# Attention's rows of maxima loaded by ACT itself, with one load moved ahead in the QKV queue and the routing's picks taken in two parts

## The chip, the cores and the metric

One core of one Trainium2 chip runs the whole program. The metric is the device time of one execution in microseconds (us). A measurement of this kernel can tell a difference of about 1% from no change.

## The reference

All arithmetic is float32. Input x is (4, 512, 512): 2,048 tokens of 512 features.

```python
x = x + 0.5 * ffn(layernorm(x))      # 8 experts, the best 2 by gate logits, relu(x W_e + b_e), mean of the two
x = x + attention(layernorm(x))      # 32 heads of 16, ALiBi bias, causal softmax, then Wout
x = x + 0.5 * ffn(layernorm(x))      # the same experts again

# attention: qkv = clip(x Wqkv^T, -8, 8); q, k = layer_norm(q), layer_norm(k)
# scores = q k^T / 4 + slope * (k_pos - q_pos), masked above the diagonal; softmax; times v; times Wout^T
# ffn: logits = x W_gate + b_gate; top 2 experts of 8; mean of relu(x W_e + b_e) over the two
```

## The kernel before, in words

The order of work on every engine is written out by hand; each engine has one queue of instructions, and semaphores order them across engines. SP issues the plain transfers, POOL the indirect ones (gather of token rows, scatter-add of results). Stages in order of time: routing 1 with the weights' split into high and low parts (about 0 to 88 us), experts 1 (to 235), QKV projection (to 430), attention (to 720), routing 2 with the output projection (to 836), experts 2.

**QKV** goes over 16 tiles of 128 tokens. In tile t DVE (`unit`, L478) first takes the statistics of x of tile t+2 (L485), so it waits for that tile's load. SP's `step` (L310) for tile t does three things in order: `store_qk(t-2)` (L301, four stores of 256 KB), `load_x(t+3)` (L293, 256 KB), `store_v(t)` (L297, 512 KB). From tile 8 to 11 each step is followed by `load_fixed` and `load` (L207, L218), which bring the q and k stacks of one of attention's first four groups (14 transfers).

**Attention** goes over 32 groups n of 4 heads, and in each over five units u. PE computes scores twice: query-major two groups ahead (`scores`, L715), of which DVE takes row maxima (`reduce`, `combine`); and key-major (`scores_by_key`, L746), of which ACT takes exponentials (`exps`, L851). The maxima enter the key-major product as extra rows of the q stack: POOL splits them into high and low parts (`split_max`, L666), PE turns them (`turn_max`, L737), ACT copies them to SBUF (`copy_max`, L845, behind the second unit's exponentials), and SP moves them by four transfers of 4 KB into two rows in each half of the stack (`max_rows`, L631). `scores_by_key(n+1, 0)` waits for these transfers (L749). In SP's loop over n (L648) stand, in order: the stack's load for group n+4, the values' load for n+2, `max_rows(n+1)`, every second time the store of results, and in groups 16 to 24 an early transfer for routing 2 (`route.sync_early`, L660, mostly 512 KB of expert weights).

**Routing** normalises eight pairs of tiles (DVE), transposes them (PE, L1295; ACT copies, L1390), multiplies by the gate (PE `gate`, L1302), adds the bias (ACT `logits_out`, L1395) and turns the logits to one PSUM bank (PE `turn_logits`, L1311). When all 16 tiles are there, DVE picks the two experts by a chain of 16 dependent instructions over 128 columns (L1492 to L1507); PE then ranks the tokens (L1362), DVE computes the slots, and the experts' gathers start.

Of the kernel before, what the change touches and what calls it, by code (L numbers as in the profile page):

```python
# [12 lines left out]
F32 = mybir.dt.float32  # L13
# [217 lines left out]
def qkv_block(nc, block, st, x1, w_turned, w_out, wo_stage, ln_params, q_dram, k_dram, v_dram):  # L231
# [4 lines left out]
    with ExitStack() as ctx:  # L236
# [334 lines left out]
def attention_block(nc, block, st, last_turns, freed, route, oT, wo_stage, v_dram, o_dram, wo_turned):  # L571
# [4 lines left out]
    with ExitStack() as ctx:  # L576
# [4 lines left out]
        part = [m.sb(f"part{i}", [P, 2, 2, SEGS]) for i in range(2)]  # L581
        m_parts = [m.sb(f"m_parts{i}", [P, 2, 4, SEGS], F32R) for i in range(2)]
        m_rows = [m.sb(f"m_rows{i}", [2 * HG, SEQ], F32R) for i in range(2)]
# [22 lines left out]
        wo_tr, wo_out = m.sem("wo_tr"), m.sem("wo_out")  # L606
        STACK_LOADS, FIXED_LOADS = 8, 6

        def ring_unit(k):

            return s_ps[k % 2]
# [4 lines left out]
        @block.sync  # L616
        def _(sp):
            def load(n):
                at_least(sp, st_done, T_UNITS * (n - SLOTS + 1))
                if n == AHEAD:  # L620
                    for par in range(2):
                        sp.wait_ge(st.v_stored[par], 16 * (TILES // 2))
                        sp.wait_ge(st.qk_stored[par], STORES * (TILES // 2))
                st.load(sp, n)

            def load_v(n):
                at_least(sp, pv_done, n - RING + 1)
# [19 lines left out]
            max_rows(0)  # L647
            for n in range(NG):  # L648
                if n + AHEAD < SLOTS:
                    st.load_fixed(sp, n + AHEAD)  # L650
                if n + AHEAD < NG:
                    load(n + AHEAD)
                if n + 2 < NG:
                    load_v(n + 2)
                if n + 1 < NG:
                    max_rows(n + 1)
                if n >= 3 and n % 2 == 1:
                    store(n - 2)
                if NG // 2 <= n < NG // 2 + EARLY_LOADS:
                    route.sync_early(sp, n - NG // 2)  # L660
            route.sync_next(sp)
            store(NG - 1)

        @block.gpsimd
        def _(pool):
            def split_max(n):  # L666
                pool.wait_ge(comb_done, n + 1)
                at_least(pool, mT_done, n - 1)
                flat = part[n % 2][:, :, :, :].rearrange("p a b s -> p (a b) s")
                nc.gpsimd.tensor_copy(m_parts[n % 2][:, 0, :, :], flat).then_inc(m_hi_done, 1)  # L670
                pool.wait_ge(m_hi_done, n + 1)
                nc.gpsimd.tensor_tensor(m_parts[n % 2][:, 1, :, :], flat, m_parts[n % 2][:, 0, :, :].bitcast(F32),
                                        ALU.subtract).then_inc(m_lo_done, 1)
# [30 lines left out]
        def _(pe):  # L704
# [32 lines left out]
            def turn_max(n):  # L737
                pe.wait_ge(m_lo_done, n + 1)
                bank = ring_unit(6 * (n + 1) + 1)
                at_least(pe, red_done, S_UNITS * (n + 1))  # L740
                for i, seg in enumerate((0, 4, 6, 5)):
                    last = nc.tensor.matmul(bank[0:2 * HG, i * P:(i + 1) * P], m_parts[n % 2][:, :, :, seg], ident_r[:, :],
                                            start=True, stop=True)
                last.then_inc(mT_done, 1)

            def scores_by_key(n, u):  # L746
                slot = n % SLOTS
                if u == 0:
                    pe.wait_ge(m_loaded[n % 2], 64 * (n // 2 + 1))  # L749
                e = 2 * (T_UNITS * n + u)  # L750
# [94 lines left out]
        def _(act):  # L845
            def copy_max(n):
                act.wait_ge(mT_done, n + 1)
                at_least(act, m_loaded[n % 2], 64 * (n // 2))
# [15 lines left out]

            copy_max(0)
            for r in range(C):
                act.wait_ge(wo_tr, r + 1)
# [5 lines left out]
            for n in range(NG):  # L873
# [133 lines left out]
def route_block(nc, m, tables, ex, x_in, xn_dram, acc, w_gate, b_gate, w_e, b_e, freed=None, o_dram=None, wo_turned=None, o_rows=None,  # L1007
# [58 lines left out]
    lg_ps = t_ps[0] if proj else wq_ps[3]  # L1066
    lgT = work[0:E, 0:2 * P]
    root = route_ps[:, 0:4]
# [19 lines left out]
    slot_lo = tables.sb("slot_lo", [P, 2 * TILES])  # L1088
    at_col = tables.sb("at_col", [P, COL_RING, P], BF16)
    at_tile = tables.sb("at_tile", [P, 2 * TILES, 3, TAB], BF16)  # L1090
# [19 lines left out]
    ln_chain, chain_sem = m.sem("ln_chain"), m.sem("chain")  # L1110
    picked_done, rank_done, onehot_done, ids_done = (m.sem(n) for n in ("picked_done", "rank_done", "onehot_done", "ids_done"))
    token_done = m.sem("token_done")
    wo_hi_done, wo_lo_done = m.sem("wo_hi_done"), m.sem("wo_lo_done")
# [134 lines left out]
    def gpsimd(pool):  # L1248
# [9 lines left out]
        for n in range(TILES):  # L1258
            pool.wait_ge(w_hi_done, n + 1)
            if n == TILES - 1:  # L1260

                pool.wait_ge(picked_done, 1)
            nc.gpsimd.tensor_tensor(ex.w_lo[:, 2 * n:2 * n + 2, :], ex.w_lo[:, 2 * n:2 * n + 2, :].bitcast(F32),  # L1263
# [66 lines left out]
    def tensor(pe):  # L1330
        pe.wait_ge(ident_done, 1)
        pe.wait_ge(g_loaded, 16)
        for u in range(PAIRS + 2):
# [25 lines left out]
        pe.wait_ge(const_done, 12)  # L1359
        pe.wait_ge(picked_done, 1)  # L1360
        both = pair[:, :, :, :].rearrange("p t k e -> p (t k e)")
# [91 lines left out]
    def vector(dve):  # L1453
# [35 lines left out]
        dve.wait_ge(const_done, 12)  # L1489
        dve.wait_ge(gate_done, PAIRS)  # L1490
        three = [P, TILES, E]
        for k, source in enumerate((logits, rest)):  # L1492
            chain(nc.vector.tensor_reduce(best[:, :, 0], source[:, :, :], X_AXIS, ALU.max))
            chain(nc.vector.tensor_tensor(eq[:, :, :], source[:, :, :], best[:, :, :].to_broadcast(three), ALU.is_equal))
            chain(nc.vector.scalar_tensor_tensor(val[:, :, :], eq[:, :, :], -100.0, n_expert[:, :, :], ALU.mult, ALU.add))
            chain(nc.vector.tensor_reduce(low[:, :, 0], val[:, :, :], X_AXIS, ALU.min))
            chain(nc.vector.tensor_tensor(pick[k][:, :, :], val[:, :, :], low[:, :, :].to_broadcast(three), ALU.is_equal))
            if k == 0:

                chain(nc.vector.scalar_tensor_tensor(rest[:, :, :], pick[0][:, :, :], NEG, logits[:, :, :], ALU.mult, ALU.add))  # L1500


        chain(nc.vector.tensor_tensor(picked[:, :, :], pick[0][:, :, :], pick[1][:, :, :], ALU.add))
        chain(nc.vector.scalar_tensor_tensor(val[:, :, :], picked[:, :, :], -100.0, n_expert[:, :, :], ALU.mult, ALU.add))
        chain(nc.vector.tensor_reduce(low[:, :, 0], val[:, :, :], X_AXIS, ALU.min))
        chain(nc.vector.tensor_tensor(pair[:, :, 0, :], val[:, :, :], low[:, :, :].to_broadcast(three), ALU.is_equal))
        nc.vector.tensor_tensor(pair[:, :, 1, :], picked[:, :, :], pair[:, :, 0, :], ALU.subtract).then_inc(picked_done, 1)  # L1507

# [292 lines left out]
```

## Time and profile before

| what | value |
|---|---|
| median of 3 runs | 975.37 us (970.96 to 982.41) |
| the profiled execution: its time, its span | 983.81 us, 982.0 us |
| PE busy, DVE, ACT, POOL | 841.5 us (86%), 632.4 (64%), 449.1 (46%), 446.1 (45%) |
| SP's hardware queue | 95,328 packets, 126.40 MB, 46.6% of 16 DMA engines |
| mean granted TensorE clock | 0.923 |

The span runs from the first to the last instruction. PE's busy time is modelled from pipelined matmuls, so a share of 86% does not say that PE never waits. ACT issues no transfer in this kernel: the profile has SP's queue and POOL's. SP's transfer instructions are listed with engine SPq, and their duration is that of issuing, not of moving the data.

### The profile page before, as it was taken

The numbers are of one execution on the slowest core, as the hardware profiler recorded it, in microseconds if no ns is written. First come the engines' busy times: TensorE is split into PE (matmuls) and PEld (weight loads), VectorE is DVE, ScalarE is ACT, GpSimd is POOL, SyncE is SP. The second block draws the span as 40 slices with busy tenths as digits, with TensorE's granted clock in tenths as the row PEclk, the third lists the DMA queues.
The fourth block names the chain that finished last, engine by engine and source line by source line (L and its number), as shares of the span: only waits on it lengthen the run. The fifth ranks groups of instructions, "written<-read, shape, count | busy, mean of one in ns | idle before, by whom it ended". The sixth has DMA issues, their size and how long they took to land. (4 is left out here: it accounts for less than half of the span.)

```text
span 982.0 us, 18936 instructions
## 1 busy us (share of the span) xinstructions
PE 841.5 (86%) x5922; PEld 592.5 (60%) x5923; DVE 632.4 (64%) x1289; ACT 449.1 (46%) x834; POOL 446.1 (45%) x565
## 2 busy tenths in 40 slices
PE   3666999993989998878899999889989983899995
PEld 1344888872677777655455555445557752788874
DVE  7966344333978877776688887678728768344432
ACT  3541333332244443347577777577754430233331
POOL 7732677764022222224243344235446431577764
PEclk9785999996899999978899999899999995899998
DMA  9985677863264689665667679898239940578874
GB/s 341 387 300 175 124 148 145 149 118 53 54 197 150 196 199 230 195 196 127 146 139 154 143 154 189 165 192 178 54 107 321 323 161 32 123 144 152 149 133 62
DMA packets 113255, 164.54 MB, mean 168 GB/s; under 512 B 16929, under 2 KB 74401, under 8 KB 112897
## 3 DMA queue, kind: packets, MB, share of 16 engines
q1 hardware_dynamic: 95328, 126.40, 46.6%
q0 software_dynamic: 17856, 37.25, 20.4%
q8 instruction: 39, 0.64, 0.3%
q14 instruction: 32, 0.25, 0.1%
HBM read 100.05 MB, written 68.68 MB: 172 GB/s over the span
## 5 line engine op out<-in xcount | busy, mean ns | idle before, releaser
L901 DVE TENSOR_REDUCE att_part<-att_s_ps 128x2 f32<-128x1024 f32 (+2 forms) x160 | 195.2, 1225 | 46.4 <-PE att_s_ps L733 42.4
L858 ACT ACTIVATE att_prob<-att_st_ps 128x512 f32<-128x512 f32 x320 | 174.2, 598 | 75.3 <-PE att_st_ps L758 71.2
L687 POOL TENSOR_SCALAR_AFFINE_SELECT att_prob<-att_prob 128x256 f32<-128x256 f32 (+1 forms) x224 | 93.7, 442 | 108.0 <-ACT att_prob L858 107.9
L153 PE MATMUL exp_z_ps<-ex_w_hi,exp_xT_hi 128*128 x312 | 132.4, 424 | 1.7 <-issue 1.3
L155 PE MATMUL exp_z_ps<-ex_w_hi,exp_xT_lo 128*128 x312 | 124.8, 400 | 0.0
L154 PE MATMUL exp_z_ps<-ex_w_lo,exp_xT_hi 128*128 x312 | 124.7, 400 | 0.0
L1684 ACT ACTIVATE exp_y<-exp_y 128x512 f32<-128x512 f32 x72 | 45.5, 632 | 170.5 <-DVE exp_y L1703 142.0
L1691 DVE TENSOR_TENSOR exp_xT_lo<-exp_t_ps,exp_xT_hi 128x512 fp32r<-128x512 f32 x78 | 53.9, 692 | 99.8 <-ACT exp_xT_hi L1675 81.2
L1263 POOL TENSOR_TENSOR ex_w_lo<-ex_w_lo,ex_w_hi 128x1024 fp32r<-128x1024 f32 x32 | 77.0, 2418 | 78.0 <-ACT ex_w_hi L1404 41.6
L771 PE MATMUL att_pv_ps<-att_prob,att_v_sb 128*32 128x256 f32 (+2 forms) x1280 | 103.2, 397 | 1.6 <-ACT wt_w_turned L863 1.6
L153 PE MATMUL qkv_o_ps<-qkv_w_hi,qkv_xT_hi 128*128 128x512 f32 x192 | 82.6, 430 | 2.4 <-DVE qkv_xT_lo L464 1.6
L154 PE MATMUL qkv_o_ps<-qkv_w_lo,qkv_xT_hi 128*128 128x512 f32 x192 | 78.6, 409 | 0.0
L155 PE MATMUL qkv_o_ps<-qkv_w_hi,qkv_xT_lo 128*128 128x512 f32 x192 | 78.0, 406 | 0.0
L1640 POOL DMA_INDIRECT out<-exp_y,ex_row_of x39 | 61.9, 1588 | 34.5 <-DMA out<-exp_y,ex_row_of 12.9
L363 POOL TENSOR_TENSOR st_partq<-qkv_wholeq,st_partq 128x512 fp32r<-128x512 f32 x16 | 20.7, 1293 | 124.9 <-ACT st_partq L435 124.9
L153 PEld LDWEIGHTS exp_z_ps<-ex_w_hi,exp_xT_hi 128*128 128x128 f32 x312 | 61.0, 195 | 15.7 <-issue 4.7
L155 PEld LDWEIGHTS exp_z_ps<-ex_w_hi,exp_xT_lo 128*128 128x128 f32 x312 | 60.0, 192 | 14.4
L1640 POOL DMA_INDIRECT acc<-exp_y,ex_row_of x33 | 52.4, 1589 | 33.4 <-issue 16.9
L154 PEld LDWEIGHTS exp_z_ps<-ex_w_lo,exp_xT_hi 128*128 128x128 f32 x312 | 60.5, 194 | 10.8
L712 PE MATMUL att_s_ps<-st_masks 64*128 64x256 bf16 (+1 forms) x640 | 58.9, 264 | 4.2 <-DVE att_part L901 4.2
L1675 ACT ACTIVATE exp_xT_hi<-exp_t_ps 128x512 fp32r<-128x512 f32 x78 | 45.4, 582 | 36.3 <-PE exp_t_ps L1652 36.3
L712 PEld LDWEIGHTS att_s_ps<-st_masks 64*128 64x128 bf16 x640 | 18.9, 97 | 61.5 <-issue 53.6
(206 smaller groups left out, 1618.2 us busy)
## 6 DMA issues: line engine op xcount, KB each, us to landing
ex_w_lo<-in_L_ffn_W_e SPq DMA_DIRECT2D x32, 512.0 KB, 6.7
v_vals<-st_vals SPq DMA_DIRECT2D x16, 512.0 KB, 2.9
q_parts<-st_partq SPq DMA_DIRECT2D x32, 256.0 KB, 3.6
k_parts<-st_partk SPq DMA_DIRECT2D x32, 256.0 KB, 4.0
att_v_sb<-v_vals SPq DMA_DIRECT2D x32, 256.0 KB, 3.8
ex_bias<-in_L_attn_hidden_states SPq DMA_DIRECT2D x8, 512.0 KB, 7.4
acc<-ex_bias SPq DMA_DIRECT2D x8, 512.0 KB, 8.3
xn<-ex_rows SPq DMA_DIRECT2D x8, 512.0 KB, 5.5
```

The lines of the kernel that those rows point to most:

```text
L153: nc.tensor.matmul(out, x_hi[:, s], w_hi(c), start=(c == 0), stop=False)
L154: nc.tensor.matmul(out, x_hi[:, s], w_lo(c), start=False, stop=False)
L155: last = nc.tensor.matmul(out, x_lo[:, s], w_hi(c), start=False, stop=(c == C - 1))
L687: last = nc.gpsimd.affine_select(out=block, in_=block, compare_op=ALU.is_ge, fill=0.0, base=0, pattern=[[0, block.shape[1]], [1, P]], chan ...
L712: nc.tensor.matmul(blocks_of(banks[half], where), mine[:, 0, :], rhs, start=(c == 0), stop=False, skip_group_check=True)
L771: last = nc.tensor.matmul(pv_ps[VW * h:VW * (h + 1), j * P + c0:j * P + c1], v_sb[n % RING][:, j, VW * h:VW * (h + 1)], prob[n % 2][:, col ...
L858: nc.scalar.activation(prob[n % 2][:, col:col + 512], st_ps[(e + half) % 3][:, :], ACT.Exp).then_inc(exp_done, 1)
L901: nc.vector.tensor_reduce(out, src, X_AXIS, ALU.max, negate=True).then_inc(red_done, 1)
L1263: nc.gpsimd.tensor_tensor(ex.w_lo[:, 2 * n:2 * n + 2, :], ex.w_lo[:, 2 * n:2 * n + 2, :].bitcast(F32), ex.w_hi[:, 2 * n:2 * n + 2, :].bitc ...
L1640: nc.gpsimd.indirect_dma_start(out=acc[:, :], out_offset=bass.IndirectOffsetOnAxis(ap=ex.row_of[:, s:s + 1], axis=0), in_=y[s % RING], in_ ...
L1684: nc.scalar.activation(y[r], y[r], ACT.Relu, scale=0.25).then_inc(y_done, 1)
L1691: nc.vector.tensor_tensor(xT_lo[r % 2][:, :], t_ps[r % 2][:, :], xT_hi[r % 2][:, :].bitcast(F32), ALU.subtract).then_inc(lo_done, 1)
```

## The change

Four edits. (1) In attention the rows of maxima are moved by ACT's own queue: two transfers a group (each takes four rows of 2 KB to two rows of the stack) in place of SP's four, given out behind the third unit's exponentials; the high and low parts stand in another order in `m_parts`, so that POOL's two instructions write with one more dimension. (2) In QKV's `step`, `load_x` stands ahead of `store_qk`. (3) In the routing the picks of tiles 0 to 13 are taken from an SBUF copy of their logits as soon as these are there, and those of tiles 14 and 15 after; for that PE's `turn_logits` of the seventh pair stands ahead of the last pair's transposes. (4) The turned logits and the one-hot columns share a tile of their own, `turning`, so that picks may begin while logits still come in.

```diff
             def step(t, par):
+                if not (isinstance(t, int) and t + 3 >= TILES):
+                    load_x(t + 3, 1 - par)
                 if after(t, 2):
                     store_qk(t - 2, par)
-                if not (isinstance(t, int) and t + 3 >= TILES):
-                    load_x(t + 3, 1 - par)
                 store_v(t, par)
...
-            def max_rows(n):
-                sp.wait_ge(m_rows_done, n + 1)
-                for half, base in halves():
-                    for part_of in range(2):
-                        row = base + SCORE_ROWS + part_of
-                        src = m_rows[n % 2][4 * part_of + 2 * half:4 * part_of + 2 * half + 2, :]
-                        sp.dma_start(q_st[n % SLOTS][row:row + 1, :, :].bitcast(F32), src.bitcast(F32)).then_inc(m_loaded[n % 2], 16)
...
-                if n + 1 < NG:
-                    max_rows(n + 1)
...
+                whole, parts = part[n % 2][:, :, :, :], m_parts[n % 2]
+                nc.gpsimd.tensor_copy(parts[:, :, 0, :, :], whole).then_inc(m_hi_done, 1)
...
+            def max_rows(n):
+                act.wait_ge(m_rows_done, n + 1)
+                for half, base in halves():
+                    row = base + SCORE_ROWS
+                    src = m_rows[n % 2][HG * half:HG * (half + 1), :]
+                    nc.scalar.dma_start(q_st[n % SLOTS][row:row + MAX_ROWS, :, :].bitcast(F32), src.bitcast(F32)).then_inc(m_loaded[n % 2], 16)
...
                 exps(n, 1)
                 if n + 1 < NG:
                     copy_max(n + 1)
-                for u in range(2, T_UNITS):
+                exps(n, 2)
+                if n + 1 < NG:
+                    max_rows(n + 1)
+                for u in range(3, T_UNITS):
                     exps(n, u)
...
+            if u == PAIRS:
+
+                turn_logits(u - 2)
             if 1 <= u <= PAIRS:
                 transpose(2 * u - 2)
                 transpose(2 * u - 1)
-            if u >= 2:
+            if u >= 2 and u != PAIRS:
+                if u == PAIRS + 1:
+                    pe.wait_ge(lg_kept, 1)
                 turn_logits(u - 2)
...
+        dve.wait_ge(gate_done, PAIRS - 1)
+        nc.vector.tensor_copy(kept[:, 0:TILES - 2, :], logits[:, 0:TILES - 2, :]).then_inc(lg_kept, 1)
+        dve.wait_ge(lg_kept, 1)
+        picks(0, TILES - 2, kept)
         dve.wait_ge(gate_done, PAIRS)
...
+        picks(TILES - 2, TILES, logits)
```

`picks(t0, t1, first)` is the chain of 16 instructions of before, on the columns of tiles t0 to t1.

## Rows read from the trace of the kernel before

**Rows 1.** Busy time by stage: us, then PE, PEld, DVE, ACT, POOL, clock, DMA share, GB/s.
```profile
480.00:550.00 70.00, 64.80 (x792) 35.39 (x792) 54.28 (x64) 49.35 (x95) 25.98 (x71) 0.95 0.65 144
640.00:720.00 80.00, 72.85 (x904) 39.27 (x900) 58.92 (x73) 60.50 (x116) 36.37 (x89) 1.00 0.61 125
```

**Rows 2.** The rows of maxima: SP's issues (ns min/median/max) and who waited (us, times).
```profile
L637 SPq DMA_DIRECT2D att_q_st<-att_m_rows x64: 558/559/657, 478.7 to 713.4; - x64
...
  PEld att_st_ps L758: 14.1, 10
```

**Rows 3.** Timeline of one undisturbed group and the next: start, us, engine, line, [idle before].
```profile
520.54 0.57 ACT L849 ACTIVATE att_m_rows<-att_s_ps 8x512 fp32r<-8x512 f32 x1
521.13 2.38 SPq L637 DMA_DIRECT2D st_q<-att_m_rows  x4
522.16 1.08 ACT L858 ACTIVATE att_prob<-att_st_ps 128x512 f32<-128x512 f32 x2 [1.05 <-PE att_st_ps L758]
523.79 2.29 ACT L858 ACTIVATE att_prob<-att_st_ps 128x512 f32<-128x512 f32 x4 [0.55 <-PE att_st_ps L758]
525.92 0.39 PE L758 MATMUL att_st_ps<-st_q,st_k 64*128 64x512 f32 x2
528.81 0.57 ACT L849 ACTIVATE att_m_rows<-att_s_ps 8x512 fp32r<-8x512 f32 x1
```

**Rows 4.** Timeline of the group with the longest wait for the rows of maxima.
```profile
621.34 2.38 SPq L637 DMA_DIRECT2D att_q_st<-att_m_rows  x4
...
629.57 0.29 PEld L758 LDWEIGHTS att_st_ps<-att_q_st,att_k_st 64*128 64x128 f32 x2 [3.49 <-DMA att_q_st<-att_m_rows]
```

**Rows 5.** Busy time by stretches of 4 us around that wait, columns as in rows 1.
```profile
622.00:626.00 4.00, 4.00 (x58) 2.22 (x56) 3.47 (x3) 2.98 (x6) 1.18 (x3) 1.00 1.07 164
...
630.00:634.00 4.00, 4.00 (x28) 2.22 (x26) 1.23 (x1) 2.17 (x5) 0.41 (x1) 0.50 0.88 146
```

**Rows 6.** Waits in QKV for the load of x: us in total, times, longest us.
```profile
DVE qkv_stats L485 <- DMA qkv_x<-acc: 14.0, 5, 4.2
```

**Rows 7.** Timeline of DVE in QKV, the statistics that open a tile's work.
```profile
286.62 0.69 DVE L485 BATCH_NORM_STATS2 qkv_stats<-qkv_x 128x6 f32<-128x512 f32 x1 [2.44 <-DMA qkv_x<-acc]
...
349.51 0.68 DVE L485 BATCH_NORM_STATS2 qkv_stats<-qkv_x 128x6 f32<-128x512 f32 x1
364.15 0.69 DVE L485 BATCH_NORM_STATS2 qkv_stats<-qkv_x 128x6 f32<-128x512 f32 x1 [4.18 <-DMA qkv_x<-acc]
...
400.86 0.69 DVE L485 BATCH_NORM_STATS2 qkv_stats<-qkv_x 128x6 f32<-128x512 f32 x1 [3.33 <-DMA qkv_x<-acc]
```

**Rows 8.** Timeline of SP's queue in QKV, one load of x and what stands ahead.
```profile
356.07 0.98 SPq L308 DMA_DIRECT2D q_parts<-st_partq  x2
358.49 2.03 SPq L295 DMA_DIRECT2D qkv_x<-acc  x1
```

**Rows 9.** Busy time by stretches of 10 us in QKV, columns as in rows 1.
```profile
360.00:370.00 10.00, 8.68 (x41) 6.57 (x39) 4.99 (x13) 4.28 (x10) 2.56 (x2) 1.00 1.05 276
```

**Rows 10.** Timeline of the end of routing 1 (PE, ACT, DVE).
```profile
59.95 0.29 PE L1315 MATMUL route_g_ps<-ex_ident,route_work 8*128 8x8 f32 x2
...
59.03 0.47 ACT L1400 ACTIVATE route_work<-route_wq_ps,route_bg 8x256 f32<-8x256 f32 x1 [2.55 <-PE route_wq_ps L1307]
...
63.59 0.29 DVE L1493 TENSOR_REDUCE route_best<-route_g_ps 128x16 f32<-128x128 f32 x1 [5.38 <-PE route_g_ps L1315]
...
71.34 0.17 DVE L1511 TENSOR_TENSOR route_counts<-route_totals 128x8 f32<-128x8 f32 x1
```

**Rows 11.** Timeline of the end of routing 2 (PE and DVE).
```profile
804.29 1.11 PE L1281 MATMUL route_t_ps<-ex_ident,wo_turned 128*128 128x128 f32 x8 [1.54 <-DVE wo_turned L1484]
...
803.69 1.00 DVE L1484 TENSOR_SCALAR wo_turned<-wt_w_turned,route_mv,route_rstd 128x512 f32<-128x512 f32 x2
810.60 0.29 DVE L1493 TENSOR_REDUCE route_best<-route_g_ps 128x16 f32<-128x128 f32 x1 [5.91 <-PE route_g_ps L1315]
...
815.46 0.29 DVE L1507 TENSOR_TENSOR route_pair<-route_eq,route_pair 128x128 bf16<-128x128 f32 x1
```

More of the change, by code:

```diff
@@ L581, in attention_block @@
         part = [m.sb(f"part{i}", [P, 2, 2, SEGS]) for i in range(2)]
-        m_parts = [m.sb(f"m_parts{i}", [P, 2, 4, SEGS], F32R) for i in range(2)]
+        m_parts = [m.sb(f"m_parts{i}", [P, 2, 2, 2, SEGS], F32R) for i in range(2)]
         m_rows = [m.sb(f"m_rows{i}", [2 * HG, SEQ], F32R) for i in range(2)]
@@ L607, in attention_block @@
         STACK_LOADS, FIXED_LOADS = 8, 6
+        MAX_LOADS = 16 * 2
         def ring_unit(k):
@@ L668, in split_max @@
                 at_least(pool, mT_done, n - 1)
-                flat = part[n % 2][:, :, :, :].rearrange("p a b s -> p (a b) s")
-                nc.gpsimd.tensor_copy(m_parts[n % 2][:, 0, :, :], flat).then_inc(m_hi_done, 1)
+                whole, parts = part[n % 2][:, :, :, :], m_parts[n % 2]
+                nc.gpsimd.tensor_copy(parts[:, :, 0, :, :], whole).then_inc(m_hi_done, 1)
                 pool.wait_ge(m_hi_done, n + 1)
-                nc.gpsimd.tensor_tensor(m_parts[n % 2][:, 1, :, :], flat, m_parts[n % 2][:, 0, :, :].bitcast(F32),
+                nc.gpsimd.tensor_tensor(parts[:, :, 1, :, :], whole, parts[:, :, 0, :, :].bitcast(F32),
                                         ALU.subtract).then_inc(m_lo_done, 1)
@@ L741, in turn_max @@
                 for i, seg in enumerate((0, 4, 6, 5)):
-                    last = nc.tensor.matmul(bank[0:2 * HG, i * P:(i + 1) * P], m_parts[n % 2][:, :, :, seg], ident_r[:, :],
+                    last = nc.tensor.matmul(bank[0:2 * HG, i * P:(i + 1) * P], m_parts[n % 2][:, :, :, :, seg].rearrange("p a k b -> p (a k b)"), ident_r[:, :],
                                             start=True, stop=True)
@@ L865, in _ @@
             copy_max(0)
+            max_rows(0)
             for r in range(C):
@@ L1066, in route_block @@
     lg_ps = t_ps[0] if proj else wq_ps[3]
-    lgT = work[0:E, 0:2 * P]
     root = route_ps[:, 0:4]
@@ L1088, in route_block @@
     slot_lo = tables.sb("slot_lo", [P, 2 * TILES])
-    at_col = tables.sb("at_col", [P, COL_RING, P], BF16)
+    turning = tables.sb("turning", [P, 2 * P])
+    lgT = turning[0:E, :]
+    at_col = turning[:, :].bitcast(BF16).rearrange("p (r n) -> p r n", r=COL_RING)
     at_tile = tables.sb("at_tile", [P, 2 * TILES, 3, TAB], BF16)
@@ L1359, in tensor @@
         pe.wait_ge(const_done, 12)
-        pe.wait_ge(picked_done, 1)
+        pe.wait_ge(picked_done, 2)
         both = pair[:, :, :, :].rearrange("p t k e -> p (t k e)")
@@ L1489, in vector @@
         dve.wait_ge(const_done, 12)
-        dve.wait_ge(gate_done, PAIRS)
[L1491 to L1500, printed above, removed]
@@ L1503, in vector @@
[L1503 to L1507, printed above, removed]
+        kept = over[:, :, :].rearrange("p e t -> p (e t)").rearrange("p (t e) -> p t e", e=E)
@@ new lines, in picks @@
+        def picks(t0, t1, first):
+            n, three = slice(t0, t1), [P, t1 - t0, E]
+            for k, source in enumerate((first, rest)):
+                chain(nc.vector.tensor_reduce(best[:, n, 0], source[:, n, :], X_AXIS, ALU.max))
+                chain(nc.vector.tensor_tensor(eq[:, n, :], source[:, n, :], best[:, n, :].to_broadcast(three), ALU.is_equal))
+                chain(nc.vector.scalar_tensor_tensor(val[:, n, :], eq[:, n, :], -100.0, n_expert[:, n, :], ALU.mult, ALU.add))
+                chain(nc.vector.tensor_reduce(low[:, n, 0], val[:, n, :], X_AXIS, ALU.min))
+                chain(nc.vector.tensor_tensor(pick[k][:, n, :], val[:, n, :], low[:, n, :].to_broadcast(three), ALU.is_equal))
+                if k == 0:
+                    chain(nc.vector.scalar_tensor_tensor(rest[:, n, :], pick[0][:, n, :], NEG, first[:, n, :], ALU.mult, ALU.add))
+            chain(nc.vector.tensor_tensor(picked[:, n, :], pick[0][:, n, :], pick[1][:, n, :], ALU.add))
+            chain(nc.vector.scalar_tensor_tensor(val[:, n, :], picked[:, n, :], -100.0, n_expert[:, n, :], ALU.mult, ALU.add))
+            chain(nc.vector.tensor_reduce(low[:, n, 0], val[:, n, :], X_AXIS, ALU.min))
+            chain(nc.vector.tensor_tensor(pair[:, n, 0, :], val[:, n, :], low[:, n, :].to_broadcast(three), ALU.is_equal))
+            nc.vector.tensor_tensor(pair[:, n, 1, :], picked[:, n, :], pair[:, n, 0, :], ALU.subtract).then_inc(picked_done, 1)
```

8 lines of the change are left out of this document (4 added, 4 removed).

## The prediction, made before the changed kernel was run

> **What bounds the kernel now.** I read the page's busy shares first, then busy time by stage, then the waits, and then timelines of the three stages that the change touches.
>
> By stage, attention is PE's: 64.80 of 70 us in its early and 72.85 of 80 in its late part, ACT next with 49.35 and 60.50 [rows 1]. An undisturbed group takes 8.27 us (ACT copies maxima at 520.54 and at 528.81) [rows 3]. The waits then show what makes groups longer: ten times PE's weight loads waited for the rows of maxima, 14.1 us together [rows 2]. In the worst group SP gave the rows out at 621.34 to 623.72, and PE started at 629.57 after 3.49 us of idleness [rows 4], while in the undisturbed one issue at 521.13 served a product at 525.92 without a wait [rows 3]. The DMA engines were full there (share 1.07), and the clock afterwards was granted at half, 1.2 in place of 2.4 GHz, for 4 us [rows 5].
>
> In QKV, DVE waited five times, 14.0 us in all, for the load of x [rows 6]: once early (2.44 us) and in each of the last four tiles that still load ahead; one such tile took from 349.51 to 364.15, which is 10.46 us and a wait of 4.18 [rows 7]. SP gave the load out at 358.49, behind stores begun at 356.07 [rows 8], and the DMA engines' share was 1.05 at 276 GB/s [rows 9].
>
> In the routing DVE idles while the last pair's logits are made, 5.38 us in routing 1 [rows 10] and 5.91 in routing 2 [rows 11], and then runs its 16 picks: 810.60 to 815.75, 5.15 us, 0.324 us apart [rows 11]. Everything behind waits for these.
>
> **The load of x moved ahead.** It passes `store_qk`, four transfers of 256 KB, and is given out up to 2.42 us earlier (356.07 for 358.49) [rows 8]. The stores wait behind one issue, 2.03 us at most [rows 8]; POOL and ACT wait for them two tiles later only, at 10.46 us a tile, so I cost that at nothing; were that cover gone, it would be 2 us on two or three tiles. What the load gains: the early wait of 2.44 us should go, since there only the stores stood in its way. In the last four tiles the engines were full, so an order alone cannot remove the work: ahead of the last x, which came at 400.86 [rows 7], stands one round of stores less, 1.05 MB at 276 GB/s [rows 9], so I take 3.8 us of the 11.6 there. Bounds: 0 and 14.0. Sum for this edit: 2.4 + 3.8 = **6.2 us**.
>
> **The rows of maxima on ACT.** Removed from SP: four issues a group, 2.38 us [rows 3], and SP's wait for ACT's copy. Queued behind that wait stood the next group's eight stack loads, the values' load, the store and the early weights; they now start up to half a group earlier, and the next thing that holds SP is the values' buffer. Nobody waits for them earlier than before.
>
> Added to ACT: two issues a group. No transfer of ACT is in the trace, so I bound its price by SP's rows: 0.559 us each [rows 2], 1.12 us a group. They come behind the third unit's exponentials (522.16 to 523.24); the next ones began at 523.79, behind 0.55 us of idleness for PE [rows 3]. Behind the waiting ACT are queued those of the fourth and fifth units, for which PE and POOL wait. The two exponentials of a unit take 1.08 us together, though one alone takes about 0.6: the second is handed over before the first has ended [rows 3]. If ACT is then free to issue, 1.12 us fit from about 522.65 to 523.77. Bounds a group: 0 and 1.12 - 0.55 = 0.57 us, times 31. I take 0, the row of overlapping exponentials being the nearest.
>
> The landing: issue starts some 1.5 us later than SP's (522.65 for 521.13), but two issues end with 523.77 where four ended with 523.51 [rows 3], and the product at 525.92 was not delayed then. So undisturbed groups stay at 8.27 us.
>
> In the ten disturbed groups the wait was for transfers that stood in one queue behind SP's loads, on full engines [rows 5]. On a queue of their own the rows need not stand behind them. That the wait goes has no row; bounds 0 and 14.1 us. I take 11, leaving 0.3 us each, because even the worst group's rows would only need to come 3.49 us earlier of the 8 that they took [rows 4]. With the wait go 4 us at half clock, 2 us of work [rows 5]: **13 us**. What is late next in such a group is ACT's first exponential, as in the undisturbed one.
>
> The Trainium skill, "DMA: Bandwidth & Descriptors", § Queues, rings and completion order, says that each engine takes turns between the queues by packets, which would let ACT's rows pass. The same page, § Issuing engines are not separate DMA queues, says that issuing from several engines saves issue time only; by it the 13 us would be 0, and that is the second rival below. No row decides: SP issued both.
>
> POOL's two instructions of `split_max` write the same 28 columns with one dimension more; the wait of PE for them is on the path, so 0 to 0.1 us a group, and I take 0. `turn_max` reads the same 8 columns.
>
> **Picks in two parts.** A step costs 0.324 us over 128 columns, of which 0.29 is the instruction [rows 11]; over 8 columns the instruction took 0.17 [rows 10]. In between, 112 columns cost 0.274 + 0.034 = 0.31, 16 columns 0.21. So the first part is a copy and 16 steps, 17 x 0.31 = 5.2 us, the second 16 x 0.21 = 3.4. In routing 2 DVE is free at 804.69; the seventh pair's logits can be turned while PE waits 1.54 us for DVE before 804.29 [rows 11]. First part to 809.9, before the last logits at 810.60; second to 814.0 in place of 815.75: 1.8 us, on the path. In routing 1 PE now waits for ACT's 0.47 us at 59.03 before the last transposes, where it turned those logits at 59.95 behind them [rows 10]: the last pair comes about 1 us later (64.6 for 63.59), and the first part runs from 59.95 to 65.2, the second to 68.6, where the old chain ended at 63.59 + 5.15 = 68.7. So 0.1 us. Bounds for both together: -2 (two pairs of transposes late, nothing hidden) and 3.5. Sum: **1.9 us**. The shared tile adds no wait, since its writes follow all reads.
>
> **The sum.** 6.2 + 13 + 1.9 = 21.1 us. The profiled execution took 983.81 us (1.8 us beside its span of 982.0) and would take 962.7. It stands 8.4 us above the median of 975.37; if its waits are what makes it slow, the new median is 962.7, if not, 954.3. I take about the middle, **958 us**. This case reaches from 946 (all upper bounds, 14.0 + 16.1 + 3.5 = 33.6 us: 950 off the profiled time, 942 off the median) to 971 (2.4 us in QKV, 6 of the 13, none in the routing: 975 and 967).
>
> **Rivals.**
>
> *ACT is held, and by more than its idleness.* If ACT issues only when its exponentials have ended, and each issue also waits for one of SP's, 2 x 2 x 0.559 = 2.24 us a group, less 0.55, delay the fourth unit's exponentials and PE behind them: 1.69 x 31 = 52 us. Against the 21.1 gained: 1015 off the profiled time, 1006 off the median, **slower**. It decides from (21.1 + 9.8)/31 = 1.00 us a group on. For it: PE has little idleness to give [rows 1], and the fifth unit's product follows the fourth's exponentials. Against it: the overlap of the exponentials [rows 3].
>
> *ACT is held by the bare issues*, 0.57 x 31 = 17.7 us: 980 or 972, **the same**. The Trainium skill, "Advanced Engine Details and Errata", § Sequencer Loop, says that engine instructions can be queued while a control instruction executes, against both; no run of ACT's transfers shows it yet.
>
> *The DMA engines are full, and the rows come as late as before.* The 13 us fall away, 8.1 remain: 976 or 967, say 971, **the same** or just faster. For it: share 1.07 in the worst group [rows 5]; against it: 4 KB a transfer are little work, and the undisturbed group's came in time [rows 3].
>
> *The moved load does not do what it says*, since the engines, not the order, set when x comes [rows 9]: 6.2 us fall away, 969 or 960.5, mostly **faster**.
>
> **How the numbers follow.** Forecast 0.47, ACT held and more 0.07, ACT held 0.16, rows as late 0.20, moved load idle 0.10. A measurement tells about 1% from no change, here 965.6 and 985.1. Faster: 0.95 of 0.47, 0.8 of 0.10, 0.4 of 0.20 and a little of 0.16, together 0.62; slower 0.08; the same 0.30. The range reaches from 944 to 979, taking in the second and third rival and leaving out the slow one; the forecast's own is 946 to 971.
>
> **What would show it.** Right: no wait of PE for the rows of maxima over 0.5 us; ACT's idleness before the fourth unit's exponentials gone down by no more than it had, and groups at 8.3 us also from 595 to 670; DVE's waits for x half or less; picks of routing 2 ending 3.4 us after the last logits. Wrong: groups longer than 8.5 us throughout with ACT's issues in front of the fourth unit; waits for the rows from 595 us on; x still late by 2 us or more in four tiles; a longer routing 1.

## The result, and the profile after

The change made the kernel **slower**: 1014.94 us against 978.25, medians of four runs each side, ratio 1.0359 with a 95% interval of 1.0311 to 1.0408. Some executions run a per cent or more slower than the others of their kernel (one of after took 1027.61 us), and ratios and intervals leave these out, so that a ratio can differ a little from that of the medians. The profiled execution of after took 1013.65 us with a span of 1011.9, which is 29.9 us more than the span of before. The mean granted clock is 0.925 where it was 0.923, so the loss is not one of the clock over the whole span.

Where the time went shows in milestones of the two traces: ACT's first copy of maxima moved by 1.0 us (437.1 to 438.1), its last by 32.4 (711.0 to 743.4), the first product of routing 2's ranks by 31.4 (815.89 to 847.29), the end by 29.9. So attention alone, from first copy to last, went from 273.9 to 305.3 us; the other stages gave back 1.5.

Attention by stage, columns as in [rows 1]:

```profile
480.00:550.00 70.00, 63.61 (x798) 34.41 (x796) 54.97 (x65) 50.50 (x97) 26.63 (x72) 1.00 0.67 138
550.00:640.00 90.00, 78.43 (x930) 42.20 (x926) 64.72 (x76) 59.23 (x113) 31.38 (x85) 0.94 0.70 146
640.00:720.00 80.00, 65.97 (x731) 35.44 (x728) 50.03 (x59) 46.30 (x88) 27.46 (x67) 0.87 0.71 141
```

No engine took over from PE: in 640 to 720 us all five are less busy than before, PE by 6.9 us and ACT by 14.2, and the clock fell from 1.00 to 0.87. PE waited, and the view of the rows of maxima, which answers to [rows 2], names for what:

```profile
L847 ACTq DMA_DIRECT2D st_q<-att_m_rows x32: 619/620/1247, 438.8 to 712.6; - x32
...
  PEld att_st_ps L749: 43.4, 25
```

The wait that the change was forecast to end went from 14.1 us in 10 groups to **43.4 us in 25** of 32. One of the 25 makes 8.04 us by itself: it comes in the second group, while SP gives out the first eight groups' stacks and their fixed rows, and it ends 10.4 us behind the last of ACT's two issues, which ended at 451.62:

```profile
451.00 0.62 ACTq L847 DMA_DIRECT2D st_q<-att_m_rows  x1
...
461.98 0.29 PEld L749 LDWEIGHTS att_st_ps<-st_q,st_k 64*128 64x128 f32 x2 [8.04 <-DMA st_q<-att_m_rows]
```

The group that answers to [rows 3], in ACT's queue, SP's queue and PE (start, us, engine, line, idle before):

```profile
520.03 0.57 ACT L840 ACTIVATE att_m_rows<-att_s_ps 8x512 fp32r<-8x512 f32 x1
521.16 0.60 ACT L856 ACTIVATE att_prob<-att_st_ps 128x512 f32<-128x512 f32 x1 [0.56 <-PE att_st_ps L749]
521.16 0.63 ACTq L847 DMA_DIRECT2D st_q<-att_m_rows  x1
521.83 0.62 ACTq L847 DMA_DIRECT2D st_q<-att_m_rows  x1
522.79 2.29 ACT L856 ACTIVATE att_prob<-att_st_ps 128x512 f32<-128x512 f32 x4 [0.55 <-PE att_st_ps L749]
...
525.08 0.19 PEld L749 LDWEIGHTS att_st_ps<-st_q,st_k 64*128 64x128 f32 x2 [0.20 <-DMA st_q<-att_m_rows]
```

Read ACT first. Its two issues, 0.62 us each, lie beside its exponentials: the one of 521.16 starts with an exponential that takes 0.60. The fourth unit's exponentials begin at 522.79 after 0.55 us of idleness for PE, the very idleness of before. **ACT is not held.** The Trainium skill, "Advanced Engine Details and Errata", § Sequencer Loop, says that engine instructions are queued while a control instruction runs; this row agrees. Then read PE: rows issued by 522.45 came just too late for 525.08. In the groups around it the wait alternates: 1.45 us at 517.10, 0.20 here, 1.20 at 534.34, 0.31 at 542.42, 1.28 at 551.67. SP's queue shows what alternates, here later and worse:

```profile
632.86 0.51 SPq L1161 DMA_DIRECT2D ex_w_lo<-in_L_ffn_W_e  x1
...
637.92 0.51 SPq L1161 DMA_DIRECT2D ex_w_lo<-in_L_ffn_W_e  x1
...
641.72 0.42 SPq L228 DMA_DIRECT2D st_k<-k_parts  x1
642.59 0.62 ACTq L847 DMA_DIRECT2D att_q_st<-att_m_rows  x1
643.24 0.62 ACTq L847 DMA_DIRECT2D att_q_st<-att_m_rows  x1
650.01 0.29 PEld L749 LDWEIGHTS att_st_ps<-att_q_st,att_k_st 64*128 64x128 f32 x2 [3.71 <-DMA att_q_st<-att_m_rows]
```

Without the turn for the rows, SP's loop gave out two groups in one burst: from 632.86 to 642.14 two weights of 512 KB, 16 stack loads of 64 and 128 KB (768 KB a group) and a values' load of 256 KB, 2.9 MB in 9.3 us. That asks for some 310 GB/s; in this stretch the engines moved 217 at a share of 1.00, so some 0.9 MB of the burst (an estimate from these two) was still to come when the rows were given out. ACT's two transfers of 8 KB, given out at 642.59 and 643.24, were still awaited at 650.01. The Trainium skill, "DMA: Bandwidth & Descriptors", § Queues, rings and completion order, has the engines take turns between queues, by which one would expect the rows to pass; here 16 KB on a queue of their own took 6.15 us behind the second issue. The same page of the Trainium skill, § Issuing engines are not separate DMA queues, says that transfers share the 16 engines whoever starts them; that is the one that the trace bears out, though how the turns went it does not show.

After such a burst comes the opposite, a pause with the clock at half (columns as above):

```profile
670.00:674.00 4.00, 1.21 (x8) 0.75 (x8) 0.62 (x2) 0.37 (x1) 1.03 (x3) 0.79 0.62 96
674.00:678.00 4.00, 4.00 (x30) 1.96 (x28) 1.68 (x3) 2.26 (x5) 1.12 (x3) 0.50 0.00 0
```

PE did little for 4 us, then worked 4 us at 1.2 GHz while the DMA engines moved nothing at all (0.00): SP gave out nothing between 669.07 and 678.26, when the next store of results let it go on.

QKV's wait, which answers to [rows 6], and routing 2's picks, which answer to [rows 11]:

```profile
DVE qkv_stats L485 <- DMA qkv_x<-acc: 13.4, 4, 5.2
```

```profile
837.84 1.00 DVE L1494 TENSOR_SCALAR wo_turned<-wt_w_turned,route_mv,route_rstd 128x512 f32<-128x512 f32 x2
838.76 0.27 DVE L1522 COPY route_over<-route_g_ps 128x112 f32<-128x112 f32 x1
...
843.86 0.17 DVE L1505 TENSOR_REDUCE route_best<-route_g_ps 128x2 f32<-128x16 f32 x1
...
846.97 0.17 DVE L1518 TENSOR_TENSOR route_pair<-route_eq,route_pair 128x16 bf16<-128x16 f32 x1
```

x waited once less, 13.4 us for 14.0. The picks' first part fills the idleness of 5.91 us: from the end of DVE's last normalisation to the first rank product it is 8.45 us (838.84 to 847.29) where it was 11.20 (804.69 to 815.89), so 2.75 us came back there. A step cost what was forecast, 0.31 us over 112 columns and 0.21 over 16; the last logits were ready by 5.0 us behind that normalisation at the latest, where it was 5.9, and that is nearly all of the 0.95 us that was not forecast.

### The profile page after: what moved, and what is told of

Same layout as the page of the kernel before. It is cut to its first block and busy times, and to the rows that moved or that the text cites. A ratio compares the mean times of both kernels' runs of the same rounds, so it can differ in the third digit from the quotient of the medians.

```text
span 1011.9 us, 18908 instructions
## 1 busy us (share of the span) xinstructions
PE 839.6 (83%) x5922; PEld 588.3 (58%) x5923; DVE 645.9 (64%) x1323; ACT 449.6 (44%) x834; POOL 446.1 (44%) x565
## 5 line engine op out<-in xcount | busy, mean ns | idle before, releaser
L762 PE MATMUL att_pv_ps<-att_prob,att_v_sb 128*32 128x256 f32 (+2 forms) x1280 | 106.1, 407 | 1.6 <-ACT wt_w_turned L861 1.6
L153 PEld LDWEIGHTS exp_z_ps<-ex_w_hi,exp_xT_hi 128*128 128x128 f32 x312 | 60.3, 193 | 13.8 <-issue 3.0
L155 PEld LDWEIGHTS exp_z_ps<-ex_w_hi,exp_xT_lo 128*128 128x128 f32 x312 | 59.4, 190 | 14.1
L749 PE MATMUL att_st_ps<-st_q,st_k 64*128 64x128 f32 (+3 forms) x256 | 37.8, 354 | 25.1 <-DMA st_q<-att_m_rows 22.4
```

What stands on the lines that cost most here:

```text
L153: nc.tensor.matmul(out, x_hi[:, s], w_hi(c), start=(c == 0), stop=False)
L155: last = nc.tensor.matmul(out, x_lo[:, s], w_hi(c), start=False, stop=(c == C - 1))
L762: last = nc.tensor.matmul(pv_ps[VW * h:VW * (h + 1), j * P + c0:j * P + c1], v_sb[n % RING][:, j, VW * h:VW * (h + 1)], prob[n % 2][:, col ...
```

## The experiments

**Theory.** SP's turn for the rows did two things beside giving them out: it put them ahead of the next loads, and it held SP to one group's loads per group. Taking it away lets bursts of loads meet the rows. **Rivals:** ACT's issues delay ACT or come too late; the rows lose on a queue of their own, whatever SP does; another part of the change did it. Every ratio below is against the kernel before, run again beside it on the same chip.

**The three parts, each alone on the kernel before.**

```
e1_qkv     load_x(t + 3) ahead of store_qk(t - 2); nothing else
e2_rows    attention's edit alone (max_rows on ACT, two transfers)
e3_picks   routing's edit alone
```

> The kernel before with one edit of the change alone: in QKV the load of x stands ahead of the stores. The prediction's step says 6.2 us gained (ratio 0.994). The trace of the whole change shows only 2.1 us gained between QKV's start and attention's first scores, with waits for x still 13.4 us: if that is this edit's own effect, the ratio is 0.997 to 1.000 and the waits for x stay above 10 us; if the picks or the rows disturb it, the waits fall below 8 us here.

> The kernel before with attention's edit alone: ACT gives out the rows of maxima, two transfers a group; QKV and routing as before. If this edit is the cause of all the loss, the ratio is 1.03 to 1.04, the waits for the rows are about 43 us in 25 groups as with the whole change, and 31 us are lost between the first and the last copy of maxima. If the other edits share in it, the ratio is under 1.02.

> The kernel before with the routing's edit alone: picks in two parts. The prediction's step says 1.9 us gained, nothing in routing 1 and 1.8 in routing 2. The trace of the whole change has the ranks of routing 1 begin 1.6 us later and routing 2 1.1 us shorter: then the ratio is within 0.999 to 1.002.

Measured: e1_qkv 1.0022 (0.9988 to 1.0056); e2_rows 1.0441 (1.0372 to 1.051), with 47.7 us of waits for rows in 22 groups and 37.4 us lost between first and last copy; e3_picks 0.9973 (0.9938 to 1.0009). So the loss lies in attention's edit alone. For e1_qkv, DVE's waits and two stretches:

```profile
DVE qkv_stats L485 <- DMA qkv_x<-acc: 12.6, 4, 4.4
```

```profile
365.00:385.00 20.00, 15.15 (x67) 11.76 (x66) 13.02 (x40) 7.31 (x17) 4.22 (x4) 0.93 1.06 180
385.00:405.00 20.00, 17.61 (x79) 14.07 (x79) 12.29 (x31) 6.90 (x16) 3.24 (x3) 0.90 1.06 262
```

The early wait of 2.44 us went, as forecast, and the first late one fell from 4.18 us to 1.05; but the next two rose to 4.37 and 4.40, and the last x, which came at 400.86 [rows 7], came at 400.59. The engines' share was 1.06 for these 40 us; that an earlier x there only makes a stack load later, for which the tile after pays, fits this, but no run shows it apart. That the move gains nothing is shown by all the traces: the stretch from QKV's first statistics (L485) to attention's first copy took 179.9 to 183.6 us in the eleven with x moved, and 180.4 to 183.3 in the five without. The copy that opens attention came at 437.3, for 437.1.

**SP gives the two transfers**, at the old place; all else as in the change.

```
-            nc.scalar.dma_start(q_st[...][row:row + MAX_ROWS, :, :], src)   # in ACT, behind exps(n, 2)
+            sp.dma_start(q_st[...][row:row + MAX_ROWS, :, :], src)          # in SP, behind load_v(n + 2)
```

> The whole change, except that SP gives out the two transfers of the rows, at the place in its queue where its four stood. If the loss lies in who gives them out and where they stand against the stack loads, this is no slower than before: ratio 0.985 to 1.000, groups at 8.3 us and waits for the rows of 14 us or less. If it lies in the two transfers being longer or laid out otherwise, the waits stay near 43 us and the ratio near 1.03.

Measured: 0.9876 (0.9814 to 0.9938), 964.95 us, the best of all; attention 257.9 us. The waits for rows that are left:

```profile
PEld att_st_ps L759 <- DMA st_q<-att_m_rows: 0.6, 2, 0.3
```

Same transfers, same sizes, same layout: who gives them out, and what that does to SP, makes 5% of the kernel.

**SP is held again, ACT still issues.** A wait in SP's loop behind `load_v(n + 2)`:

```
e4_landed  + sp.wait_ge(m_loaded[(n + 1) % 2], MAX_LOADS * ((n + 1) // 2 + 1))   # rows of n + 1 have landed
e5_paced   + sp.wait_ge(m_rows_done, n + 2)                                      # ACT has copied the next maxima
```

> The whole change, and SP waits, at the place where its four transfers stood, until ACT's two rows of the next group have landed, before it goes on to the next stack load. Theory of order (SP, no longer held in step, gives the stack loads of two groups in one burst ahead of the rows, and the rows come behind them): the loads now follow the rows, waits for the rows fall from 43 to under 15 us, ratio 0.99 to 1.005. Rival of the late issue or of a slow ACT queue: waits stay above 30 us, ratio above 1.02.

> The whole change, and SP waits at the same place only until ACT has copied the maxima, so that it is held in step, but its loads start just ahead of ACT's rows instead of behind them. If the burst of two groups' loads is what costs, the waits halve, to some 20 us, ratio about 1.015. If the order alone costs, every group now has loads ahead of its rows: waits of 1 to 2 us in nearly all 31 groups, 40 us, ratio 1.03 or more.

Measured: e4_landed 1.0057 (1.0025 to 1.009), with 14.7 us in 10 groups, the numbers of the kernel before:

```profile
  PEld att_st_ps L751: 14.7, 10
```

So this one wait in SP's loop (e4_landed) takes back 28.7 of the 29.3 us of added waits. It does both things that the theory names: it holds SP in step, and it puts the loads behind the rows. e5_paced had 27.2 us in 19 groups, between its two cases; its runs spread from 984.52 to 1011.22 us, median 1004.04, and give no interval, and the trace is of one of 1001.17, so it decides nothing by itself.

**ACT issues sooner**, right behind its copy of the maxima, SP free as in the change:

```
-                exps(n, 2)
                 if n + 1 < NG:
                     max_rows(n + 1)
-                for u in range(3, T_UNITS):
+                for u in range(2, T_UNITS):
```

> The whole change, but ACT gives out the rows right behind its copy of the maxima, ahead of the third unit's exponentials, SP not held in step. Rival of the late issue: the rows go out about 0.6 us earlier, which removes the waits that are below that, about 10 of 43 us, ratio 1.025; if the issue is the whole cause, ratio below 1.01. Theory of order: in the groups of the burst the waits stay at 2 to 4 us; ratio 1.02 to 1.035.

Measured: 1.0368 (1.0294 to 1.0443); the trace, of its shortest execution (1000.91 us, median 1014.54), has 27.8 us of waits in 15 groups. ACT's issues start 0.6 us behind the start of the copy, where the change's start 1.1 to 1.6 behind in most groups and 2.7 at most; the ratio stayed that of the change (the rival said 1.025, or below 1.01), so the late issue is not the cause.

**No stack loads to meet**: `load` runs for the first eight groups only, so groups 8 to 31 compute on old stacks (PE's wait for the stacks is shortened to match, not shown).

```
-                if n + AHEAD < NG:
+                if n + AHEAD < SLOTS:
                     load(n + AHEAD)
```

> The whole change without the stack loads of groups 8 to 31: left out, so that these groups compute on the stacks of the first eight. Theory of order: with no loads to stand behind, no group from 10 on waits for its rows more than 0.3 us, groups are at 8.27 us, and the time is some 40 us below that of the whole change. A slow ACT queue: waits of about 1 us go on.

Measured, a single execution: groups from 505.08 to 695.37 us took 8.27 on the mean, with four waits of 0.21 to 0.75 us, all while the weights come (none over 0.3 was expected):

```profile
PEld att_st_ps L749 <- DMA st_q<-att_m_rows: 13.1, 4, 9.6
PEld att_st_ps L749 <- DMA att_q_st<-att_m_rows: 0.7, 2, 0.5
```

Of its 13.8 us of waits 9.6 are one and 2.4 another, while the first eight groups' stacks and fixed rows are loaded. ACT issues in every group, and behind these two hardly anything waits: the loads are what delays the rows. The early waits remain, and so its time, 981.87 us, is that of the kernel before with its 14.1 us, 33 below the change where some 40 were expected.

**Two transfers from SP, alone**; and ACT sooner with SP held until the rows have landed.

```
e9_two             kernel before, MAX_LOADS = 16 * 2, max_rows in SP with two transfers of two rows
e10_early_landed   e4_landed and e6_early together
```

> The whole change, with SP waiting until ACT's rows have landed before it gives out the next group's loads (as in the run of that kind before), and with ACT issuing right behind its copy of the maxima, one unit earlier. If order and the end of the issue are all that counts, the two issues end about 1.9 us after the copy, as where SP gave the two, and the kernel stands as that one: waits for the rows under 3 us in all, ratio 0.985 to 0.993. If ACT's queue is slower in itself, the waits stay at 8 us or more in all, and the ratio is 0.997 or higher.

> The kernel before, with two transfers of two rows for its four of one, given by SP at the same place; loads of x and routing as before. If the gain of the run where SP gave the two comes from these shorter issues, the waits for rows fall from 14.1 us to under 3 and the ratio is 0.985 to 0.992. If it came from the loads of x and the routing, the ratio is 0.995 to 1.0 here.

Measured: e9_two 0.9962 (0.9927 to 0.9998), 7.6 us of waits in 6 groups; e10_early_landed 1.001 (0.9979 to 1.0041), 9.8 us in 6. Shorter issues halve the waits but are not all that e7_sp_two gained, which had 0.6 us. With loads behind the rows and the early issue, ACT's rows still come later than SP's do in e7_sp_two (1.001 against 0.9876, intervals apart); but SP goes on only when the rows have landed here, and as soon as they are given out there, so the queue is not the only difference.

**Loads placed in front of the rows.** On SP's queue, and then the same with ACT's queue:

```
-                if n + AHEAD < NG:
-                    load(n + AHEAD)
                 if n + 2 < NG:
                     load_v(n + 2)
+                if n >= AHEAD:
+                    sp.wait_ge(st_done, T_UNITS * n)     # group n - 1 has its scores
+                if n + AHEAD < NG:
+                    load(n + AHEAD)
e11_loads_first   on e7_sp_two: SP gives the rows, behind these loads
e12_early_even    on e6_early: ACT gives them
e13_late_even     on the change itself: ACT, behind exps(n, 2)
```

The values' load, which has a wait of its own, thus comes ahead of the stack loads in all three.

> The kernel in which SP gives the two transfers, with the next group's eight stack loads given some 2 us later, once the group before has its scores, so that they go out in the 4 us just before the rows in place of the 4 us just behind; issuer, queue and issue times of the rows stay. If loads ahead of the rows on full engines are what delays them, the waits for rows rise from 0.6 us to 10 us or more and the ratio is 1.00 or higher. If rows given by SP land in time whatever stands ahead of them, the waits stay under 2 us and the ratio at 0.985 to 0.993.

> The whole change with ACT issuing right behind its copy of the maxima, and with SP giving each group's stack loads once the group before has its scores, one group's loads per group. It is the run with the stack loads in front of the rows, but for the queue: the rows' two issues start at about the same time behind the copy, on ACT in place of SP, with eight loads just ahead of them. If SP running ahead in bursts was the whole cost, waits for the rows stay at 10 us or less in all and the ratio at 0.985 to 1.00. If rows on a queue of their own lose against SP's loads whatever the pace, waits are 20 us or more and the ratio is 1.02 or higher, near that of the run with early issues and no pacing (27.8 us, 1.0368).

> The whole change, ACT issuing behind the third unit's exponentials as it does there, with SP giving each group's stack loads once the group before has its scores, one group's loads per group. If bursts were the whole cost, the waits fall from 43.4 us to some 15, as where SP waited for the rows to land, and the ratio to 1.00 to 1.008. If ACT's queue loses in itself, waits stay over 30 us and the ratio over 1.025.

Measured: e11_loads_first 0.9887 (0.9832 to 0.9942). Its SP queue, and its waits:

```profile
524.27 0.44 SPq L225 DMA_DIRECT2D att_q_st<-q_parts  x1
...
527.54 0.42 SPq L228 DMA_DIRECT2D att_k_st<-k_parts  x1
528.00 1.28 SPq L643 DMA_DIRECT2D st_q<-att_m_rows  x2
```

```profile
PEld att_st_ps L761 <- DMA st_q<-att_m_rows: 4.9, 3, 2.7
PEld att_st_ps L761 <- DMA att_q_st<-att_m_rows: 1.6, 4, 0.6
```

Eight loads stand right in front of the rows in every group, and the waits are 6.5 us, between the two cases of the expectation; the trace is of the longest of its four executions (979.37 us, median 972.78). Against e7_sp_two, with the loads behind the rows, that is 5.9 us more of waits and no difference in the ratio that is clear of noise. **So the half of my theory that spoke of order nearly fell:** one group's loads ahead of the rows, on one queue, cost little beside the 43.4 us. (On ACT's queue, e12_early_even against e10_early_landed, loads in front of the rows go with 7.2 us more.) What is left is the pace. e12_early_even, 1.0054 (1.0023 to 1.0084), has the same loads, and ACT's issue 0.6 us behind the start of the copy, where SP's came 1.0 behind it; with 17.0 us it too falls between its two cases:

```profile
526.46 0.42 SPq L225 DMA_DIRECT2D att_q_st<-q_parts  x1
...
527.91 1.27 ACTq L849 DMA_DIRECT2D st_q<-att_m_rows  x2
```

```profile
PEld att_st_ps L751 <- DMA st_q<-att_m_rows: 8.6, 9, 3.5
PEld att_st_ps L751 <- DMA att_q_st<-att_m_rows: 8.4, 5, 5.1
```

e13_late_even, 1.0099 (1.0059 to 1.0139), is the change with the pace, and with the values' load moved, and nothing else:

```profile
PEld att_st_ps L751 <- DMA st_q<-att_m_rows: 14.3, 6, 8.3
PEld att_st_ps L751 <- DMA att_q_st<-att_m_rows: 4.8, 4, 3.0
```

From 43.4 us to 19.1, and from 497 to 596 us not one wait, where the change waited in nearly every group: the alternation went with the bursts. Of the 19.1, 8.3 are one wait at 461.59 us, in the first groups, where this pace is not yet in force and SP gives stacks and fixed rows without a pause; it is the change's own wait at 461.98. Without these two, the pace brings 35.4 us down to 10.8. With SP paced the early issue is worth a little: 17.0 us of waits for 19.1 (e12 and e13), 9.8 for 14.7 (e10 and e4), and 0.4 to 0.5% each time, with intervals that overlap.

e12 against e11 has 10.5 us of waits more and a ratio higher by 1.7% (the intervals do not meet), with ACT's queue in place of SP's. That is not a price of the queue alone. 3.5 us are again one wait in the first groups. 5.1 us are another, where SP, which no longer waits for ACT's copy, gave out two weights of 512 KB 5.9 us apart; in e11 they came 7.7 to 8.8 apart:

```profile
616.16 0.51 SPq L1162 DMA_DIRECT2D ex_w_lo<-in_L_ffn_W_e  x1
...
622.07 0.42 SPq L1162 DMA_DIRECT2D ex_w_lo<-in_L_ffn_W_e  x1
...
631.47 0.29 PEld L751 LDWEIGHTS att_st_ps<-att_q_st,att_k_st 64*128 64x128 f32 x2 [5.06 <-DMA att_q_st<-att_m_rows]
```

The other twelve waits make 8.4 us, for 6.5 in e11's seven. Whether ACT's queue is slower in itself is not shown.

**Whether the gain adds up**: two transfers from SP and the picks, loads of x in the old order.

> The kernel before with two transfers of two rows given by SP, and with the picks in two parts; loads of x in the old order. If the parts add up, 0.9962 times 0.9973 gives 0.9935 (0.989 to 0.998). If the gain of the run that also had the load of x moved (0.9876) needs that move, this one stays above 0.992; if it does not, 0.985 to 0.991.

Measured: 0.9964 (0.9926 to 1.0001). There is no wait for rows at all in its trace, and attention takes 258.5 us, 15.4 less than before; but its first copy of maxima came at 442.7, 5.6 us later. The two executions profiled differ by 9.1 us, 983.81 and 974.68: 15.4 less in attention, less 5.6 for the later start and 0.7 behind attention. But 983.81 lies above the median of before in the runs beside this one, 981.16, and the medians are 5.9 us apart (975.3), which is 0.6%. The start of attention lies between 432.8 and 441.7 us over the ten kernels here with the change's QKV and routing, 0.9% of the whole, and most of that is there when QKV begins: its first statistics came at 251.4 to 259.5. By its own condition (above 0.992) this run would say that the gain of e7_sp_two (0.9876) needs the move of x; but that move gained nothing alone, attention is as short here as there, the intervals of the two overlap, and e7_sp_two's trace was 6.5 us ahead already at QKV's first statistics (252.9 for 259.4). So what the traces show is an earlier start; why it varies was not settled.

## Why the prediction was wrong

I forecast 958 us with a range to 979, faster at 0.62; it was 1014.94. The sign, the range and the chances were wrong.

**The step that failed** is the one for the disturbed groups: "On a queue of their own the rows need not stand behind them ... I take 11". It was a gain of 13 us in the sum; attention lost 31.4. Two things were wrong in it. The row I rested it on [rows 4, 5] shows rows that come late on full engines; it does not show that the queue was what held them, and in e11_loads_first, with one queue and the loads in front of the rows, they held them for 6.5 us in all. And three paragraphs before I had written, of SP's next loads, that they "now start up to half a group earlier ... Nobody waits for them earlier than before". True of who waits for the loads, but those loads take the engines that the rows need. I had seen that SP's wait would go and booked it as free; it was the kernel's pacing: with it gone the waits rose from 14.1 us to 43.4, and with a wait put back into SP's loop they were 14.7 (e4_landed) or 19.1 (e13_late_even).

**Its bounds failed with it**: "bounds 0 and 14.1 us". Nothing excluded a loss. In hindsight the profile of before could have given a price below nothing: all 32 groups meeting what the ten met, at 1.4 us each, is 45 us of waits, and 43.4 came. That these are so near is partly chance, since 25 groups waited and one of them for 8.04 us.

**The rate at which waits become time was right.** I added 2 us of half clock to 14.1 us, 1.14 us lost per us waited. The size of the prize was right with it: where the waits went (e7_sp_two), attention gained 16.0 us for 13.5 us of them. Attention's length over the runs:

| kernel | waits for rows, us (groups) | first to last copy, us | ratio |
|---|---|---|---|
| e14_two_picks | 0 | 258.5 | 0.9964 |
| e7_sp_two | 0.6 (2) | 257.9 | 0.9876 |
| e11_loads_first | 6.5 (7) | 265.6 | 0.9887 |
| e9_two | 7.6 (6) | 266.8 | 0.9962 |
| e10_early_landed | 9.8 (6) | 272.8 | 1.001 |
| e1_qkv | 11.1 (9) | 269.8 | 1.0022 |
| e3_picks | 13.3 (11) | 271.0 | 0.9973 |
| e8_no_loads | 13.8 (6) | 274.0 | one run |
| before | 14.1 (10) | 273.9 | 1 |
| e4_landed | 14.7 (10) | 274.8 | 1.0057 |
| e12_early_even | 17.0 (14) | 280.8 | 1.0054 |
| e13_late_even | 19.1 (10) | 278.5 | 1.0099 |
| e5_paced | 27.2 (19) | 290.3 | no interval |
| e6_early | 27.8 (15) | 293.7 | 1.0368 |
| after | 43.4 (25) | 305.3 | 1.0359 |
| e2_rows | 47.7 (22) | 311.3 | 1.0441 |

From e7_sp_two to after it is 47.4 us for 42.8, or 1.11; the other rows lie within 6 us of that line. before, e1_qkv and e3_picks have the same code in attention and show how much a single trace is worth, 11.1 to 14.1 us of waits.

**The load of x, 6.2 us:** wrong in size. The early 2.44 us went, but the later waits took it up; the 3.8 did not come, since the last x came at 400.59 for 400.86 though a round of stores no longer stood ahead of it. The rival "the moved load does not do what it says" (0.10) is what happened: 1.0022.

**ACT's issues at nothing:** right, and groups of 8.27 us with ACT issuing in each (e8_no_loads) show it too. An issue took 0.62 us where I took 0.559 from SP's rows. Neither rival that held ACT came about.

**Undisturbed groups at 8.27 us:** right where no loads meet the rows (e8_no_loads), wrong in the change, whose middle groups alternate.

**The picks, 1.9 us:** in routing 2 the forecast was 1.8 and 2.75 came. In routing 1 I forecast 0.1: the first rank product came at 68.89 before, and at 66.62, 67.16, 69.30 and 70.45 in four traces with the edit (e3_picks, e7_sp_two, e14_two_picks, after), whose clock from 50 to 72 us was 0.92, 0.89, 0.81 and 0.84; no gain or loss of the edit itself stands out of that. Over the whole kernel, 0.9973, not clear of no change.

**The rivals:** "rows as late as before" had the right doubt and priced it at nothing lost. (It is the third in the list; the paragraph on the two rules calls it the second.) The slower rival had the sign, and its 1015 us is the measured time to the microsecond, by luck: ACT was not held.

## What to carry to other kernels

A wait in a queue that you take away may be the only thing that paces what stands behind it: before booking its removal as free, list what will be given out earlier, and on which engines it meets the transfer that you want to hurry. Moving a small urgent transfer to another engine's queue did not take it past big ones here; holding the big ones to one stage's worth per stage took most of the loss back, at the price of one wait in SP's loop. And where a row shows a late transfer on full engines, ask also what it would cost if every group came as late as those few did, and let the range reach that far.

## What the runs showed of the hardware that was not expected

- Two transfers of 8 KB on ACT's queue, beside SP's burst, were awaited 6.15 us behind the end of their last issue (643.86 to 650.01), and 10.4 us in the second group (451.62 to 461.98). With an even pace, and the same eight loads just ahead, ACT's queue waited 17.0 us in all where SP's own waited 6.5; part of that is SP's other traffic, so it is no measure of the queue alone.
- An issue of two rows took ACT 0.62 us beside a running exponential, and SP 0.61 to 0.62; one row took SP 0.56. Two issues of two rows thus cost 1.24 us where four of one cost 2.24.
- PE ran from 674 to 678 us at 1.2 GHz, behind a wait of 3.81 us that ended at 672.79. The DMA engines' share in these 4 us was 0.00, so in that stretch the half clock came with PE's own idleness before it, and not with traffic.
